# Spreading the filler work of the attention phase: one item per slot instead of two in query chunks 3 and 4

## What is computed

```python
qkv = (x @ w_qkv).reshape(Bx, Lx, 3, NUM_HEADS, HEAD_DIM)
scores = einsum('bhqd,bhkd->bhqk', q, k) / sqrt(64)
scores = where(causal, finfo.min, scores)
out = einsum('bhqk,bhkd->bhqd', softmax(scores), v)
x = layernorm(x + out @ w_out)
# ternary linear: w_t = sign(w) * (|w| > 0.5 * mean|w|), x_norm = x / rms(x)
h = gelu(einsum('bsd,fd->bsf', x_norm(x), w_up_t))
x = layernorm(x + einsum('bsd,fd->bsf', x_norm(h), w_down_t))
```

## Time and profile before

| | |
|---|---|
| time, median of 2 runs | 3461.66 us (3437.95 and 3485.37) |
| profiled execution: time, and span of its slowest core | 3434.98 us, 3433.4 us |
| spans of the eight cores in it | 3423.6 to 3433.4 us |
| phase 2, from the first exp to the last (core 0) | 408 to 2139 us |
| busy share: PE, ACT, DVE | 77%, 54%, 28% |
| granted TensorE clock, mean of core 0 | 0.824 |

### The profile page before, as it was taken

One profiled execution on the slowest core, in us unless ns is written; L12 is line 12 of the kernel. 1 busy time (PEld: TensorE's weight loads), 2 busy tenths in 40 slices (PEclk: granted clock), 3 DMA queues, 4 the chain that ended last, 5 costly groups with the idle time before them and its releaser, 6 DMA issues. The chain is left out here.

```text
span 3433.4 us, 52517 instructions; the slowest of 8 cores (3423.6 to 3433.4 us)
## 1 busy us (share of the span) xinstructions
PE 2637.6 (77%) x19601; PEld 1333.7 (39%) x19808; DVE 970.8 (28%) x2483; ACT 1854.7 (54%) x2165; POOL 115.7 (3%) x231
## 2 busy tenths in 40 slices
PE   5996465767777777777778788334599999999998
PEld 2443122333333343343344444122344444444444
DVE  5443353443322222322211111454411111111111
ACT  2543023556576677877887887355444434443443
POOL 0000000000000000000000000000000000000000
PEclk9998667778767679879887755656699999999999
DMA  7666201010101101001000000343311111111111
GB/s 133 154 156 138 47 1 50 18 51 7 50 14 33 30 1 38 26 1 38 26 1 13 26 14 1 123 150 108 89 46 32 47 47 46 31 47 47 46 31 37
DMA packets 54922, 171.26 MB, mean 50 GB/s; under 512 B 6545, under 2 KB 6546, under 8 KB 54674
## 3 DMA queue, kind: packets, MB, share of 16 engines
q1 hardware_dynamic: 37730, 134.33, 12.5%
q0 software_dynamic: 16944, 33.56, 6.8%
HBM read 167.87 MB, written 33.55 MB: 59 GB/s over the span
## 5 line engine op out<-in xcount | busy, mean ns | idle before, releaser
L38 ACT ACTIVATE p_sb<-sc,negC 128x1024 bf16<-128x1024 f32 (+3 forms) x1152 | 1159.5, 1041 | 519.5 <-PE pvB L38 502.0
L38 PE MATMUL sc<-QT,KT 64*128 64x512 bf16 (+3 forms) x2304 | 530.2, 452 | 184.4 <-ACT p_sb L38 180.9
L38 PE MATMUL dwn<-wdnT,hTs 128*128 128x512 bf16 x1984 | 450.5, 380 | 17.3 <-ACT hTs L38 15.3
L38 PE MATMUL upq<-wupT,x1Ts 128*128 128x512 bf16 x2015 | 452.4, 380 | 8.6 <-DVE x1Ts L38 2.4
L38 PE MATMUL pvA<-VS,p_sb 128*128 128x65 bf16 x4224 | 373.4, 215 | 31.2 <-DVE p_sb L38 18.1
L38 PE MATMUL pvB<-VS,p_sb 128*128 128x65 bf16 x4224 | 376.4, 216 | 7.4 <-DVE attO L38 7.4
L38 PEld LDWEIGHTS pvA<-VS,p_sb 128*128 128x128 bf16 x4224 | 219.6, 106 | 367.9 <-issue 363.0
L38 ACT ACTIVATE h_sb<-upq,r_all 128x512 bf16<-128x512 f32 x256 | 175.2, 685 | 228.1 <-PE upq L38 225.0
L38 PEld LDWEIGHTS upq<-wupT,x1Ts 128*128 128x128 bf16 x2048 | 198.6, 98 | 256.9 <-issue 24.1
L38 PEld LDWEIGHTS dwn<-wdnT,hTs 128*128 128x128 bf16 x2048 | 195.9, 98 | 233.5 <-issue 15.4
L38 PEld LDWEIGHTS sc<-QT,KT 64*128 64x128 bf16 x2304 | 132.8, 96 | 358.6 <-issue 329.1
(11 more groups left out here) (107 smaller groups left out, 1876.7 us busy)
## 6 DMA issues: line engine op xcount, KB each, us to landing
wr<-w_up SPq DMA_DIRECT2D x64, 512.0 KB, 5.0
wr<-w_down SPq DMA_DIRECT2D x64, 512.0 KB, 4.5
xb<-x POOLq DMA_DIRECT2D x64, 256.0 KB, 4.1
xfy<-x SPq DMA_DIRECT2D x32, 512.0 KB, 3.4
x1spill<-xfy SPq DMA_DIRECT2D x32, 512.0 KB, 2.6
x1f<-x1spill SPq DMA_DIRECT2D x32, 512.0 KB, 5.7
out<-outs SPq DMA_DIRECT2D x32, 512.0 KB, 6.5
x1b<-x1spill POOLq DMA_DIRECT2D x32, 256.0 KB, 5.2
```

What stands on the lines that cost most here:

```text
L38: getattr(self.real, op)(*args, **kw))
```

## The change

The two lists of the normalization are no longer popped in block 0, and the budget of two items per drain, so far for nj up to 20, holds only for nj up to 12. Where it is one, drains still come in every slot from 2 on for nj = 16 (chunk 3) and in every even slot for nj = 20 (chunk 4).

```diff
-                            if k == 2 and pend_ln:
+                            if k == 2 and p >= 1 and pend_ln:
                                 fn, cc2, tt2 = pend_ln.pop(0)
                                 fn(cc2, tt2)
-                            if k == 4 and pend_ln2:
+                            if k == 4 and p >= 1 and pend_ln2:
...
                                 drain_end(p - 1,
-                                          budget=(2 if nj <= 20 else 1))
+                                          budget=(2 if nj <= 12 else 1))
```

## The result

The changed kernel takes 3407.87 us (median of 27 runs, 3401.84 to 3512.5) against 3442.85 us (median of 26 runs, 3436.84 to 3565.99) of the kernel before, now measured beside it. The ratio is 0.9896, 95% interval 0.9874 to 0.9918: 1.0% faster, some 35 us, and less than the 2% beyond which a difference of this kernel was called clear in the prediction. The profiled execution took 3401.55 us against 3434.98 us.

What follows compares the result with a forecast made beforehand. ScalarE's exps were taken as the floor, its idle time in chunks 3 and 4 as winnable. Chunk 4's 22.7 and chunk 3's 8.0 us gave 30.7, so 3434.98 - 30.7 = 3404 us; range 3380 to 3448.

Steps and rivals of the forecast that it cites:

- Only chunks 3 and 4, and the first edit nothing: All direct effect lies in chunks 3 and 4, 451.7 us; the condition p >= 1 on the two lists gains 0.
- Chunk 4, 22.7 us: Chunk 4, priced block by block from chunk 5's pattern: gains sum to 22.7 us, 11.1 in 4.2, 6.4 in 4.4.
- Block 4.3, 2.6 us: Block 4.3: a new square wait at slot 2 replaces slot 4's 5.10 us wait; gain 2.6, between -2 and 4.
- Block 4.1, 2.1 us, and 4.5 to 4.7, 0.5 us: 4.1: projection halves in slots 2 and 4, gain 2.1; 4.5 to 4.7: four items in four slots, 0.5 in all.
- Chunk 3, 8.0 us: Chunk 3, one item in every slot: gains 0.8 in 3.1, 8.7 in 3.2, -1.5 in 3.3, sum 8.0 us.
- The signs named beforehand: Chunk 4 215 to 222 us, chunk 3 200 to 205, clock of 4.3 and 4.4 over 0.75, chunks 5 to 7 nearly unchanged.
- the sum of the upper ends: Upper ends of the block terms in chunks 3 and 4: about 46 us gained, so 3389.
- The clock: Chunks 3 and 4: the skill's rule says cutting bursts costs clock; the trace of single-item chunks, with higher clock, leans otherwise.
- only moved: Rival: items in chunks 3 and 4 cost ScalarE the same wherever they are; 3435 us, chance 0.08.
- half of it: Rival: overlap in 4.2 and 3.2 at about its lower ends, 4.1, 4.3, 4.4 at half clock; 3420 us, chance 0.14.
- Clock taken: Rival: without bursts TensorE is granted only 0.5 in chunks 3 and 4; 3456 us, slower, chance 0.06.
- Chunk 7 changes too: Rival: five slow blocks of chunk 7 keep the full clock, 21.5 us more gained; 3382 us, chance 0.08.

Runs made afterwards that it cites:

- e1: Kernel before, with one item per drain only for nj of 20 and over, so chunk 4 alone changes: 3411.94 us, ratio to before 0.9922.
- e2: Kernel before, with one item per drain only for nj of 16, so chunk 3 alone changes: 3434.54 us, ratio to before 0.9977.
- e4: Changed kernel plus one unused 512-column matmul in each slot of blocks 7.3 to 7.7: 3375.28 us profiled, against 3401.55.
- e5: Kernel before plus one unused 512-column matmul in each slot from 6 on of blocks 4.3 and 4.4: 3434.2 us in one execution.
- e3: Kernel before, with chunk 4's drains ending behind emit_qev so emit_qnrm comes a drain later: 3437.3 us, ratio to before 0.9997.
- e7: Changed kernel plus an unused 512-column matmul in chunks 2 to 7, slots three or more behind the last item: 3411.11 us profiled, ratio to before 0.9920.
- e8: e7 plus a pause in the drain behind the residual add of tile 3, block 2 of chunks 3 to 6: 3419.31 us, ratio to before 0.9946.

## Why the prediction was right, step by step

- *Only chunks 3 and 4, and the first edit nothing:* shown, by the lengths of chunks 5 to 7 and by e1 and e2.
- *Chunk 4, 22.7 us:* 24.1 measured. Block 4.2 was priced at 11.1 and gave 11.6; the wait for the x tile stayed, as forecast. Block 4.4 was priced at 6.4 and gave 8.0. The pattern of chunk 5 was a good model because it was the same instruction pattern. No run isolates the 11.6 us of block 4.2; that they come from the pairs taken apart is read from ScalarE's holes alone.
- *Block 4.3, 2.6 us:* 1.4. The 4.51 us wait at slot 2 was foreseen to the hundredth; missed was that `emit_qnrm` of dc 2 at slot 18, on the causal diagonal, stands behind masks that wait for exps. ScalarE has a hole of 2.78 us there on core 1, for which the sum had nothing, since the model, block 6.3, has no item on its diagonal. Block 4.2 had the same wait before (3.57 us), so part of what 4.2 gained came back here.
- *Block 4.1, 2.1 us, and 4.5 to 4.7, 0.5 us:* 0.6 and 2.6. In 4.1 it is the clock: core 0, on which I worked, had the block at 0.63 while the median core had it at 0.91, so there was little to win. In the last blocks only 4.7 has a higher clock (0.62 to 0.69, and 28.2 to 26.8 us); 4.5 and 4.6 kept theirs within 0.02 and are 0.4 and 0.8 us shorter, which stays open.
- *Chunk 3, 8.0 us:* 8.9 measured, but by other terms, so the sum came out by luck. 3.2 gave 6.9 instead of 8.7, 3.3 cost 2.3 instead of 1.5, 3.1 was priced at a gain of 0.8 and cost 0.7, and 3.4, priced at 0, cost 0.7. The rest, 4.5 us in 3.5 to 3.7, I had at nothing: their four items one to a slot run with the clock of 3.6 at 0.87 and not 0.66, which goes with 2.9 us of it. The hole at the x tile in 3.2 was 10.0 us and is still 9.01:

```profile
891.18 1.11 ACT L38 ACTIVATE p_sb<-sc,negC 128x1024 bf16<-128x1024 f32 x1 [9.01 <-PE pvB L38]
```

- *The signs named beforehand:* all came but one. Chunk 3 was to be 200 to 205 us and is 198.4; the bounds were set from core 0 (210.4 before), the longest of the eight, and the median core had 207.3. In the sum of the upper ends, one term of 2 us stands for no block; without it the end is at 3391 and not 3389, which moves nothing.
- *The clock:* that it would rise and not fall was argued from chunks 5 and 6 alone. e4 and e5 show filler as a cause of the higher clock. The rule of the Trainium skill against which it was weighed (TensorE: Matmul & The Clock Gate, section on HAM oscillation: work in one piece, for gaps bring the slow clock) is half borne out. In block 4.4 the clock does fall within the 5.10 us wait. But cutting the bursts made no more gaps of that kind: it took the one of 4.4 away and left 4.51 and 2.26 us in 4.3. And chunk 7 shows a slow clock without a gap: blocks 7.3 to 7.7, slots with only scores, exps and pv, ran at 0.50 for over 200 us, and on core 0 TensorE never idled longer than 0.87 us in them.
- *The rivals:* "only moved" and "half of it" are out by the ratio's interval. "Clock taken" is out by the rows. "Chunk 7 changes too" did not happen by itself; e4 shows that the 21.5 us I gave it can be had with filler, and more (28.1).

Two steps fell in the experiments, not in the prediction's sum: that taking `emit_qnrm` out of its pair would be enough to end the stall and lift the clock (e3), and that filler is free wherever there is no item (e7, e8).

## What to carry to other kernels

Where an engine other than TensorE sets the pace and side work is put between, spread the side work evenly over the slots, one item at a time. The picture behind this, which fits the blocks here but was not measured as a rule, is that a burst costs its length less the room of one slot, while each item alone may fit into that room. Look at the granted clock of the stretches that have no side work; if it is at half, even matmuls whose result nobody reads can pay (28 us in chunk 7), but give them nothing to wait for. And before moving an item, read what will stand ahead of it on the engine that feeds it: two of the waits met here, both of a square (behind the epilogue, and behind the masks of the diagonal), only changed their place when items moved, and the one for the x tile came up in new blocks when filler was put behind its add.

## What was not expected of the hardware

- One extra matmul of 512 columns per slot makes the slots faster: 40.7 to 34.7 us for 32 slots, granted clock 0.50 to 1.00 (e4). Without it TensorE at half clock was itself busy 35.0 of 40.6 us, and still was not granted more.
- Which block of chunks 3 and 4 runs at which clock differs between cores with the same program: 4.1 took 27.3 us on core 0 and 25.0 on the median core, chunk 3 203.9 to 210.4 us over the eight. After the change chunk 3 takes 196.5 to 202.8 us. Chunk 4 differs less, 241.1 to 244.5 us before and 217.6 to 220.0 after.
- In block 4.4 before, the clock fell from 1.00 to 0.50 within a TensorE wait of 5.10 us and stayed there for the 21.7 us left of the block. In e5, with one unused matmul in each slot behind the same wait, it was at 1.00 again for the last 14.8 us.
